# A decoder block on one core: the second expert layer in 64 by 32 tiles, shifts in four row groups, and half a normalisation on ScalarE

## The reference

```
attn:   q, k = x Wq', x Wk';  a = softmax(tanh(q k' / sqrt(128)));  out = a x     (over the 128 sequences, per token)
xattn:  16 heads of 8, softmax over the 64 context tokens of the same sequence, out projection Wo
ffn:    xn = layernorm(x)*gamma + beta
        logits = unit(xn)*scale . unit(mu)            [b, n, 16 experts, 16 slots]
        dispatch = softmax(logits over the 64 tokens n); combine = softmax(logits over all 256 slots)
        slot_in = einsum(bnd,bnes->besd) (xn, dispatch)
        h = gelu(slot_in w1 + b1)   (32 hidden);  slot_out = h w2 + b2
        out = einsum(besd,bnes->bnd) (slot_out, combine)
```

## Time and profile before

| | us |
|---|---|
| median of three runs | 626.12 |
| the profiled execution, and its span | 625.29, 623.5 |
| busy: TensorE, VectorE, ScalarE, GpSimd | 520.1, 410.1, 345.1, 286.9 |
| self attention with the weights' preparation | 0 to 93 |
| cross attention | 93 to 326.6 |
| `experts_in` | 326.6 to 529.3 |
| `experts_out` | 529.3 to 623.5 |

### The profile page before, as it was taken

How to read it: one execution, slowest core, us unless ns; L and a number is a source line. 1 busy time by engine, 2 the same in 40 slices (tenths; PEclk the granted TensorE clock), 3 DMA queues, 4 the chain that set the end, 5 groups by cost and what they waited for, 6 DMA issues and landing times. The chain is left out here.

```text
span 623.5 us, 19720 instructions
## 1 busy us (share of the span) xinstructions
PE 520.1 (83%) x7660; PEld 371.6 (60%) x7660; DVE 410.1 (66%) x1187; ACT 345.1 (55%) x487; POOL 286.9 (46%) x369
## 2 busy tenths in 40 slices
PE   4748867989889999999860599999999983999996
PEld 3536655555356666666640355655555552999995
DVE  5458845679988898998425657574746620577775
ACT  2525633555687888888840155656666566344440
POOL 3113303455676877877108664868687422100000
PEclk9969977999989999999995689999999996899999
DMA  6353114541001011111100011222221312445543
GB/s 181 87 178 120 76 58 129 165 137 44 2 22 38 26 36 39 31 30 40 38 20 1 0 70 54 90 68 88 72 100 59 103 56 71 132 152 150 150 149 100
DMA packets 60912, 49.30 MB, mean 79 GB/s; under 512 B 15648, under 2 KB 50592, under 8 KB 60832
## 3 DMA queue, kind: packets, MB, share of 16 engines
q1 hardware_dynamic: 60832, 48.20, 25.4%
HBM read 30.87 MB, written 17.04 MB: 77 GB/s over the span
## 5 line engine op out<-in xcount | busy, mean ns | idle before, releaser
L567 DVE TENSOR_REDUCE c_mx<-ps 128x16 f32<-128x1024 f32 x64 | 78.0, 1218 | 12.9 <-PE ps L722 12.9
L521 POOL TENSOR_TENSOR c_k_bd<-c_k,w_mask 128x512 bf16<-128x512 f32 x80 | 83.7, 1071 | 1.2 <-DVE c_work L605 1.2
L1286 PE MATMUL ps<-w_w,h_bd 128*64 128x128 f32 x1024 | 71.5, 279 | 6.3 <-DVE o_slot_out L1238 6.3
L644 ACT ACTIVATE c_work<-ps 128x2048 f32<-128x2048 f32 x32 | 60.0, 1874 | 26.8 <-PE ps L751 26.8
L1286 PEld LDWEIGHTS ps<-w_w,h_bd 128*64 128x64 f32 x1024 | 63.2, 141 | 7.2 <-DVE o_slot_out L1238 7.2
L1230 ACT ACTIVATE h_bd<-hidden 32x512 f32 (+1 forms) x64 | 40.2, 628 | 41.4 <-PE ps L1286 40.8
L1057 ACT ACTIVATE e_slot_in<-ps 128x1024 f32<-128x1024 f32 x32 | 32.8, 1024 | 51.8 <-PE ps L1115 51.8
L1262 DVE TENSOR_TENSOR o_slot_out<-ps,w_b 128x512 f32<-128x512 f32 x64 | 44.0, 687 | 20.7 <-PE ps L1286 20.3
L1000 DVE TENSOR_REDUCE e_cm<-ps 128x16 f32<-128x1024 f32 x16 | 19.6, 1225 | 49.8 <-PE ps L1125 49.8
L1115 PE MATMUL ps<-e_disp,e_xn 64*128 64x256 f32 x256 | 36.3, 400 | 9.5 <-ACT e_slot_in L1057 8.3
L654 ACT ACTIVATE c_q_bd<-x_all,w_mask 128x512 f32<-128x512 f32 x64 | 42.8, 719 | 0.0
(11 more groups left out here) (155 smaller groups left out, 1209.9 us busy)
## 6 DMA issues: line engine op xcount, KB each, us to landing
x_all<-x_scratch SPq DMA_DIRECT2D x128, 64.0 KB, 2.3
combine_scratch<-e_comb SPq DMA_DIRECT2D x16, 512.0 KB, 2.7
ctx_sb<-combine_scratch SPq DMA_DIRECT2D x16, 512.0 KB, 3.3
x_sb<-in_x SPq DMA_DIRECT2D x16, 256.0 KB, 3.7
ctx_sb<-in_ctx SPq DMA_DIRECT2D x16, 256.0 KB, 3.2
x_scratch<-a_x SPq DMA_DIRECT2D x16, 256.0 KB, 2.0
e_rden<-dispatch_inverses SPq DMA_DIRECT2D x64, 64.0 KB, 2.0
out<-o_y SPq DMA_DIRECT2D x64, 64.0 KB, 2.1
```

The source lines that it names most:

```text
L521: ins = nc.gpsimd.tensor_tensor(k_bd[:, c.m2, s, :], k32[:, c.v, :], w["mask8"][:, s:s + 1].to_broadcast([P, TOK]), ALU.mult)
L567: nc.vector.reduce_max(mx[:, c.m2, :, p], ps[:, SCORE:SCORE + 2, :].rearrange("p a (h m) -> p (a h) m", m=N), AX_X).then_inc(mx_sb.sem, 1)
L644: nc.scalar.activation(prob[:, h, :], ps[:, 0:4, :].rearrange("p a b -> p (a b)"), ACT.Exp, scale=float(HD) ** -0.5).then_inc(p_sb.sem, 1)
L1286: ins = nc.tensor.matmul(ps[64 * (g % 2):64 * (g % 2) + 64, p, at:at + D], h_bd[:, c.m2, s % 2 * PC + s // 2, g].rearrange("p e k -> p (e ...
```

## The change

- `experts_out`: the second layer uses tiles of 64 rows by 32 columns. A group's four experts are treated as two pairs; `h_bd` holds for each pair 64 rows and 32 columns. Per sequence 8 matmuls instead of 4, in eight positions of the array (two row halves by four column groups). The chunk is cut into two halves u of four sequences; bank 2u+a takes experts 8a to 8a+7. VectorE's additions of b2 follow that cut. `w1`'s output rows, `w2` and `b1` are placed so that experts 8 to 15 have their pairs in the other row half (`place`).
- `experts_in`: the maxima are turned to four row groups (twelve matmul records instead of three transposes), negated in one [128, 256] activation, and `pick` and `sel` matmuls are issued in turn, each in its own row group of 32. The masks are made by VectorE from the identity. A part of bank 5 is cleared first. The sums go to DRAM in three transfers instead of one, to undo the new placement.
- Self attention: two of the four normalised tokens of a chunk are made by ScalarE, with a shift that GpSimd prepares in two more operations.
- 29 weight loads instead of 36.

```diff
 # self_attention, GpSimd, VectorE, ScalarE
+                    nc.gpsimd.tensor_tensor(shift[:, c.m2, :], mv[:, c.m2, :, 0], neg_one[:], ALU.mult).then_inc(rooted.sem, 1)
...
+                    nc.gpsimd.tensor_tensor(shift[:, c.m2, :], shift[:, c.m2, :], rstd[:, c.m2, :], ALU.mult).then_inc(rooted.sem, 1)
...
-                    for b in range(BC):
+                    for b in range(BC // 2):
...
+                    for b in range(BC // 2, BC):
+                        ins = nc.scalar.activation(xn[:, c.m4, b, 0:D], x_sb[:, bass.ds(c.v * BC + b, 1), :].rearrange("p a d -> p (a d)"),
+                                                   ACT.Identity, bias=shift[:, c.m2, b:b + 1], scale=rstd[:, c.m2, b:b + 1])
 # weight_loads
+def place(expert):
+    return expert % 4 ^ (2 if expert >= EXPERTS // 2 else 0)
...
-    for e in range(EXPERTS):
-        loads.append((w["b2"][SLOTS * (e % 8):SLOTS * (e % 8 + 1), e // 8, :],
-                      a["L0_ffn_b2"][e:e + 1, :].to_broadcast([SLOTS, D])))
+    for e in range(8):
+        loads.append((w["b2"][SLOTS * e:SLOTS * (e + 1), :, :],
+                      a["L0_ffn_b2"].rearrange("(a e) d -> e a d", a=2)[e:e + 1].to_broadcast([SLOTS, 2, D])))
 # experts_in, SyncE
-                sp.dma_start(sums_dram[c.v].rearrange("e (r q) -> e r q", r=2), raw[0:P:HID, c.m4, :, 1, :]).then_inc(sums_out.sem, 16)
+                sp.dma_start(halves[:, :, 0, :], raw[0:P:HID, c.m4, :, 1, 0:P]).then_inc(sums_out.sem, 16)
+                sp.dma_start(halves[0:2, :, 1, :], raw[2 * HID:P:HID, c.m4, :, 1, P:2 * P]).then_inc(sums_out.sem, 16)
+                sp.dma_start(halves[2:4, :, 1, :], raw[0:2 * HID:HID, c.m4, :, 1, P:2 * P]).then_inc(sums_out.sem, 16)
 # experts_in, VectorE (GpSimd's memsets and selects of sel32 and pick32 are gone)
+        nc.vector.memset(ps[:, 5, 0:ES], 0.0).then_inc(ps_cleared, 1)
 # experts_in, TensorE
-                    nc.tensor.transpose(ps[0:SC, 5, h * P:(h + 1) * P], cm[:, c.m2, h, :], w["ident"][:])
-                nc.tensor.transpose(ps[0:SC, 5, 2 * P:3 * P], rm[:, c.m2, :], w["ident"][:]).then_inc(mT_ps.sem, 1)
+                    for g in range(2):
+                        nc.tensor.matmul(ps[64 + 32 * g:64 + 32 * g + SC, 5, h * P:(h + 1) * P], cm[:, c.m2, h, :], w["ident"][:],
+                                         start=True, stop=True)
+                for g in range(2):
+                    ins = nc.tensor.matmul(ps[32 * g:32 * g + SC, 5, 0:P], rm[:, c.m2, :], w["ident"][:], start=True, stop=True)
+                ins.then_inc(mT_ps.sem, 1)
...
+                for p in range(PC):
+                    for h in range(2):
+                        rows = slice(32 * h, 32 * h + SC)
+                        ins = nc.tensor.matmul(ps[:, 3 + h, p * P:(p + 1) * P], pick[rows, p, :], neg[rows, c.m2, 0:P],
                                                start=False, stop=True, skip_group_check=True)
...
+                    rows, q = slice(64 + 32 * (p % 2), 64 + 32 * (p % 2) + SC), p % 2 * 2 + p // 2
+                    ins = nc.tensor.matmul(ps[:, 1 + q // 2, q % 2 * ES:(q % 2 + 1) * ES], sel[rows, q, :], neg[rows, c.m2, 0:ES],
 # experts_out, TensorE
+        def layer(c, u):
...
+            for i in range(4):
+                for q in range(4):
+                    for a in range(2):
+                        g, rows = 2 * a + q // 2, 64 * (q % 2 ^ a)
+                        ins = nc.tensor.matmul(ps[32 * q:32 * (q + 1), 2 * u + a, i * D:(i + 1) * D],
+                                               h_bd[rows:rows + 64, c.m2, (i % 2) * PC + 2 * u + i // 2, g].rearrange("p e k -> p (e k)"),
+                                               w["w2"][rows:rows + 64, g, :], start=True, stop=True)
+            ins.then_inc(s_ps.sem, 1)
...
+            layer(t.plus(1), 0)
+            combine(t.plus(0), 0)
+            layer(t.plus(1), 1)
+            combine(t.plus(0), 1)
 # build
-        h_bd = kit.sb("h_bd", [P, 2, SC, 4, 4, SLOTS])
+        h_bd = kit.sb("h_bd", [P, 2, SC, 4, 2, SLOTS])
```

More of the change, by code:

```diff
@@ L383, in weight_loads @@
               (w["w1"][:], a["L0_ffn_w1"].rearrange("e d h -> d e h"))]
[L384 removed]
+    for g in range(2):
         loads.append((w["b1"][:, g:g + 1], a["L0_ffn_b1"][4 * g:4 * g + 4, :].rearrange("c (h o) -> (c h) o", o=1)))
[L386 to L389 removed]
+    loads.append((w["w2"][:, 0:2, :], a["L0_ffn_w2"][0:8].rearrange("(g c) h d -> (c h) g d", g=2)))
+    for i in range(2):
+        at, x = slice(2 * HID * (1 - i), 2 * HID * (2 - i)), slice(2 * i, 2 * i + 2)
+        for g in range(2, 4):
+            loads.append((w["b1"][at, g:g + 1], a["L0_ffn_b1"][4 * g + 2 * i:4 * g + 2 * i + 2, :].rearrange("c (h o) -> (c h) o", o=1)))
+        loads.append((w["w2"][at, 2:4, :], a["L0_ffn_w2"][8:16].rearrange("(g i c) h d -> i (c h) g d", g=2, i=2)[i]))
+    for e in range(8):
+        loads.append((w["b2"][SLOTS * e:SLOTS * (e + 1), :, :],
+                      a["L0_ffn_b2"].rearrange("(a e) d -> e a d", a=2)[e:e + 1].to_broadcast([SLOTS, 2, D])))
     return loads
@@ L1168, in _ @@
                         x, at = 4 * g + e, (g % 2) * P
-                        ins = nc.tensor.matmul(ps[HID * e:HID * (e + 1), 6 + g // 2, at:at + P].rearrange("p (r q k) -> p r q k", r=2, q=PC),
+                        ins = nc.tensor.matmul(ps[HID * place(x):HID * (place(x) + 1), 6 + g // 2, at:at + P].rearrange("p (r q k) -> p r q k", r=2, q=PC),
                                                w["w1"][:, x, :],
@@ L1186, in experts_out @@
     slot_out = kit.sb("o_slot_out", [P, 2, SC, 2, D + 1])
-    comb = landing[:].rearrange("p (a b) c d -> p a b (c d)", a=2)
+    comb = landing
     rden = kit.sb("o_rden", [P, 2, PC])
@@ L1220, in _ @@
     def _(act):
-        act.wait_ge(before.cleared, 4)
+        act.wait_ge(before.cleared, 2)
         def step(t):
@@ L1238, in _, with shift @@
         nc.vector.memset(slot_out[:, :, :, :, D:D + 1], 1.0).then_inc(zeroed, 1)
+        def shift(c, u, a):
+            if not c:
+                return
+            dve.wait_ge(s_ps.sem, s_ps.at(c, u + 1))
+            if c.plus(-2): dve.wait_ge(y_ps.sem, y_ps.at(c.plus(-2)))
+            nc.vector.tensor_tensor(slot_out[:, c.m2, 4 * u:4 * u + 4, a, 0:D], ps[:, 2 * u + a, :].rearrange("p (s d) -> p s d", s=4),
+                                    w["b2"][:, a:a + 1, :].to_broadcast([P, 4, D]), ALU.add).then_inc(s_sb.sem, 1)
         def finish(c, h):
@@ L1256, in step @@
         def step(t):
-            for p in range(PC):
-                c = t.plus(1)
-                if c:
-                    dve.wait_ge(s_ps.sem, s_ps.at(c, p + 1))
-                    if c.plus(-2): dve.wait_ge(y_ps.sem, y_ps.at(c.plus(-2)))
-                    nc.vector.tensor_tensor(slot_out[:, c.m2, 2 * p:2 * p + 2, :, 0:D],
-                                            ps[:, p, :].rearrange("p (s a d) -> p s a d", s=2, a=2),
-                                            w["b2"][:].rearrange("p (o a) d -> p o a d", o=1).to_broadcast([P, 2, 2, D]),
-                                            ALU.add).then_inc(s_sb.sem, 1)
-                if p % 2:
-                    finish(t.plus(0), p // 2)
+            shift(t.plus(1), 0, 0)
+            shift(t.plus(1), 0, 1)
+            finish(t.plus(0), 0)
+            shift(t.plus(1), 1, 0)
+            shift(t.plus(1), 1, 1)
+            finish(t.plus(0), 1)
         walk(dve, step, first, last, lo, hi)
@@ new lines, in layer @@
+        def layer(c, u):
+            if not c:
+                return
+            if c.i is None and c.k < 2 and u == 0:
+                pe.wait_ge(act_sb.sem, act_sb.at(c))
+                if c.k: pe.wait_ge(s_sb.sem, s_sb.at(c.plus(-1), 2))
+            for i in range(4):
[6 more added lines that the diff above has]
+            ins.then_inc(s_ps.sem, 1)
@@ new lines, in combine @@
+        def combine(c, h):
+            if not c:
+                return
+            if h == 0:
+                pe.wait_ge(comb_in.of(c), comb_in.at(c))
+                pe.wait_ge(s_sb.sem, s_sb.at(c))
+            elif c.plus(2):
+                pe.wait_ge(act_sb.sem, act_sb.at(c.plus(2)))
+                pe.wait_ge(s_sb.sem, s_sb.at(c.plus(1), 2))
+            if c.plus(-1): pe.wait_ge(y_sb.sem, y_sb.at(c.plus(-1), h + 1))
+            for p in range(2 * h, 2 * h + 2):
+                for r in range(2):
+                    s = 2 * p + r
+                    for a in range(2):
+                        ins = nc.tensor.matmul(ps[N * r:N * (r + 1), 4 + h, (p % 2) * (D + 1):(p % 2 + 1) * (D + 1)],
+                                               comb[:, c.m2, a, s * N:(s + 1) * N], slot_out[:, c.m2, s, a, :],
+                                               start=a == 0, stop=a == 1)
+                ins.then_inc(y_ps.sem, 1)
@@ L1321, in build @@
         hidden = kit.sb("hidden", [P, 4, S * SLOTS])
-        h_bd = kit.sb("h_bd", [P, 2, SC, 4, 4, SLOTS])
+        h_bd = kit.sb("h_bd", [P, 2, SC, 4, 2, SLOTS])
```

(2 more changed lines are left out.)

101 lines of the change are left out of this document (39 added, 62 removed).

## The result

The changed kernel takes 606.96 us (median of 4 runs, 606.19 to 611.32), the kernel before 625.63 in the same measurement: a ratio of 0.9716 (95% interval 0.966 to 0.9771). Forecast were 602.8 us and a range of 596 to 614. The profiled execution took 607.0 us, with a span of 605.2 (before 623.5), so 18.3 us are to be placed. A run more than 1.5% above the fastest of its kernel counts as slow and is left out of medians and ratios here (612.18 us of the kernel with the combine loads behind the sums, and one run of the kernel before of 1704.56). The table takes the same events in both traces; its terms add up to the 18.3.

The account below looks back on a forecast made before the run. TensorE, busy 87 of the last 94 us, was the bound, with VectorE to bound `experts_out` afterwards. The terms -13.6 - 5.0 - 2.8 + 1.8 - 3.7 = -23.3 us gave 602.8 us, range 596 to 614.

Parts of the forecast that it names:

- Second expert layer: `experts_out`: eight places cut a chunk from 5.26 to 4.35 us, VectorE becoming the bound; 13.6 us saved.
- The first rival: Second expert layer: eight places overlap only in part, 22 ns a record, 3.9 us saved, 612.5 us; chance 0.15.
- The second: Rival in `experts_out`: combine loads land in 5.2 us, 4.7 us a chunk, 8.4 saved, 608.0 us; chance 0.12.
- Third rival, the row halves take turns: Second expert layer: one row half at a time into a PSUM bank, 6.2 us a chunk, 630.4 us; chance 0.08.
- Dispatch shifts: `experts_in`: pick and select matmuls in four row groups take 0.45 us instead of 0.99; 5.0 us saved.
- Lead-in: Start of `experts_in`: mask work gone and `h_bd` clear halved, less 0.3 for a PSUM clear; 2.8 us saved.
- Sums in three transfers: End of `experts_in`: four more issues by 0.46 us for chunks 14 and 15; 1.8 us lost.
- Self attention: Seven fewer loads before the first x1 store, 3.2 us, and a shorter blocked normalisation, 0.5; 3.7 us saved.
- The bound of 0: Self attention: nothing saved if the store's landing is set by the transfers' backlog and not by its issue.
- the ring: Self attention's cycle of TensorE, tanh, exp, TensorE: 3.84 us a chunk, forecast to stay unchanged.
- The fourth rival: Outside the last stage: transposes take turns and the store lands no earlier; -14.6 us, 611.5 us; chance 0.10.
- The forecast's best case: Whole kernel, all gains at their best: -4.5 - 3.6 - 5.4 + 1.4 - 16.5, that is 597.5 us.

Follow-up runs that it names:

- the written-out kernel: Changed kernel with `experts_out` written out for all 18 steps on all four engines instead of a loop of four steps: 613.37 us, ratio 0.9807.
- the half body: Changed kernel with TensorE's `experts_out` loop body of two chunks instead of four, combine loads signalling by two semaphores: 608.33 us, ratio 0.9713.
- The four-place kernel: Changed kernel with the second expert layer using four of the eight array places, both values of a on the same row half: 630.8 us, ratio 1.0057.
- the spread loads: Changed kernel with 29 weight and 4 context loads moved from step -1 of self attention to steps 8 to 13: 599.82 us, ratio 0.9567.
- last kernel: The combined kernel with TensorE's loop of two chunks: 594.99 us, ratio 0.9515.
- the combined kernel: Changed kernel with spread loads, combine loads behind the sums and early memset together: 595.12 us, ratio 0.9523.
- both half layers first: Written-out kernel with both half layers before both combinations, two changes of tile shape a chunk instead of four: 614.01 us.
- combine loads early: Changed kernel with the first two combine loads issued in step 14 of `experts_in` (605.8 us) or behind the last load of the sums (606.88 us).
- the early memset: Kernel with combine loads behind the sums, plus the memset of `slot_out`'s ones moved to the start of `experts_in`: 603.27 us, ratio 0.9623.

## Why the forecast was right

**Second expert layer (-13.6 forecast, -9.8).** The pace of a record was right: 13.5 ns, with all eight places at work together. The bound was wrong, and that the period is 4.34 us for 4.35 is luck: two terms were off and cancelled. A change of tile shape costs 0.2 us, four times a chunk; the sum had 0.1 for the one and 1.01 us for a half layer with the other in it (measured 1.09 each for both halves). So TensorE takes 4.34 us and not 3.98, and it stays the bound. VectorE waits for it, and the 0.2 us of waits that I gave TensorE don't exist. Two terms were missing. The pauses in the first passage of the loop (2.9 us) were shown by the written-out kernel and by the half body. The clock at half behind a wait of 3.08 us (1.4 us) was shown by the kernel whose combine load lands in time. Without both the term would have been 14.1.

The four-place kernel says why there were pauses only now: at 27 ns a record there are none, at 13.5 there are. Supply of instructions is my reading of it. The page of the profile has only the transfers of the instruction queue (packets, MB, share), of the changed kernel and of the one without the loop:

```profile
q8 instruction: 59, 0.97, 0.7%
```

```profile
q8 instruction: 69, 1.13, 0.8%
```

Ten packets of 16 KB more go with the 6.4 us; when a single packet came, and which pause it ended, isn't shown. The Trainium skill (Runtime: NRT & Kernel Launch, Instruction fetch mechanics) says that instructions are streamed in blocks of 16 KiB, that crossing into the next block is mostly hidden, and that a taken branch stalls when its target isn't in the current window of two blocks, one reason to prefer full unrolling. The size agrees with the packets. The preference doesn't hold here: the loop's turns cost nothing that shows, and the unrolled stage is the slower one.

The first rival (22 ns) fell by the rows of the half layer. The second fell too: the combine loads never end a wait in the steady part.

**Third rival, the row halves take turns.** Its condition didn't hold. Its price was near for the period, 6.2 us for the 6.07 of the kernel with four places. That the totals agree (630.4 and 630.8) is partly luck: from the first combination to the end that kernel lost 11.2 us against the kernel before, not 14, and ahead of it only 4.5 were won, not 9.7. The changed kernel writes each bank from both row halves and shows the full overlap. The rule of the Trainium skill (TensorEngine Tiling (Array Packing), Restrictions and Gotchas), by which different row tiles can't use one PSUM bank at once, shows here as no cost at all.

**Dispatch shifts (-5.0, -5.08).** The mechanism came as written: L1197 starts 0.34 us after the first pick (0.45 assumed), and L1205 waits 0.19 us for `slot_in`. Timeline of TensorE:

```profile
441.16 0.23 PE L1185 MATMUL ps<-e_neg,e_pick 8*128 8x128 bf16 x2
...
441.50 0.66 PE L1197 MATMUL ps<-w_ident,e_xu 128*128 128x128 f32 x4
442.35 1.08 PE L1205 MATMUL ps<-e_slot_in,w_w 128*32 128x128 f32 x32 [0.19 <-ACT e_slot_in L1087]
```

L1205 starts 1.19 us after the first pick, where 1.22 was called the earliest. The period fell from 10.23 to 9.84 us, 0.39 a chunk for 0.33. One chunk took 10.46, and so 5.08 were left. In the other traces one or two chunks take 10.5, and in three of them a single one takes 12.2 to 13.0 (from one exponential of the combine weights to the next). The chain of the changed kernel at that place shows the reason for the first kind:

```profile
402.20 1.03 ACT e_comb L1101
403.25 0.36 SPq L942
403.65 4.24 DMA dispatch_inverses<-e_inv
...
410.81 1.54 DMA dispatch_sums<-e_raw
412.36 1.53 DMA e_sums<-dispatch_sums
```

The inverses (8 KB) go out right behind the 512 KB of the combine weights (L942) and land in 4.24 us, where 1.5 were enough at the end of the stage with nothing ahead of them. SyncE waits for them, the sums go out late, and VectorE stands at the reciprocal with all its work behind it. Before the change landings of 4.4, 4.2 and 4.1 us made no chunk late. At 10.23 us a chunk there was room for this; at 9.84 there is less, and this landing used it up. Another of 4.5 us, at 463.33, made no chunk late, so the landing alone doesn't decide it. The kernel with one transfer of the sums has a chunk of 10.49 too, so the longer issues aren't the cause. I had not forecast it, and no run tested an edit of the inverses' order.

**Lead-in (-2.8, -3.6).** The clear of `h_bd` takes 1.82 us, and L975 starts at 335.64, 6.07 us earlier than L941 did, of which 2.6 come from the stage before. So 3.4 for my 3.1, and the 0.3 for the clear of PSUM didn't show.

**Sums in three transfers (+1.8, +2.5).** 1.4 us by experiment; the cause of the rest isn't shown.

**Self attention (-3.7, -2.6).** Right in kind. The first x1 store is issued 2.0 us earlier, not 3.2, because a merged load with two parts takes longer to issue (0.66 in the row below, 0.46 for a plain one). The store also takes longer to land, 5.5 us from its issue for 5.0. So the wait of VectorE is 8.54 us instead of 10.12. The bound of 0 had named the backlog of the transfers; it is a part of the wait, as the spread loads show.

```profile
18.91 0.66 SPq L176 DMA_DIRECT2D w_w<-in_L_ffn_w  x1
```

The normalisation's half on ScalarE is worth 0.9 at most (0.5 forecast), and the ring didn't move. What I missed is the size of what was left: a reordering won 9.0 us where the merging won 2.6.

The fourth rival fell with the dispatch shifts. The forecast's best case doesn't follow its own bounds: with 5 for self attention and 0.7 for the sums they give 596.3, not 597.5.

## What to carry to other kernels

When small matmuls in many places of the array raise the pace, price every change of tile shape and the passages of code that run for the first time. Before, both products had tiles of 128 by 64 and no change of shape, and at 55 ns a record there was no pause. Now they cost 4 x 0.2 us a chunk and 3 us a stage. A wait of a few microseconds ahead of a stage can cost more than itself, because the clock may fall in it: read the granted clock behind every such wait. Before merging transfers, ask whose turn they take: moving the weight loads behind the first stores was worth over three times as much as having fewer of them.

## What the runs showed of the hardware that I had not expected

- A change between tiles of 64 x 32 and 128 x 64 costs about 0.2 us of TensorE's time: 0.22 from four against eight places, 0.20 from two combinations side by side. Two half layers side by side saved 0.05 to 0.15.
- The granted clock in the first combination fell to 0.50 in all seven traces in which TensorE had waited 2.42 us or more just ahead of it or of the half layer before it: 2.42 (four tokens on VectorE), 2.45 (last kernel), 3.04 (written out), 3.08 (changed kernel), 3.45 (one transfer of the sums), 3.49 (half body) and 4.50 (spread loads). It was 1.00 behind 0.64 (before), 1.44 (the combined kernel), 1.53 (four places), 1.56 (both half layers first) and none (combine loads early). The kernel with the early memset is the exception, 0.50 behind 1.08; its clock had been low since 518.9.
- Written-out code is not free: the same instructions without the loop took 6.2 us more in a stage of 77.
- The 8 KB of inverses, issued right behind 512 KB on the same queue, landed after up to 4.5 us (median of all 2.5), and after 1.45 with none ahead.
- The first x1 store, behind the weight and context loads, landed 5.5 us after its issue, and after 2.0 with these loads moved away.
